# Cross-attention stage: every fourth head's turned probabilities copied by DVE, behind the maximum of the pair two steps on

## The reference

```
qh, kh, vh = 16 heads of 32 features of layernorm(x), c, c      # 256 queries, 256 keys per sequence
scores = einsum('bhqd,bhkd->bhqk', qh, kh) / sqrt(32);  key > query is masked to -10000
attn   = softmax(scores);  out = einsum('bhqk,bhkd->bhqd', attn, vh)
x      = x + tanh(g_xattn[1]) * out
```

## Time and profile before

| | us |
|---|---|
| median of 3 runs | 2086.57 (2085.92 to 2087.85) |
| profiled execution, device time | 2086.45 |
| profiled execution, span of the trace | 2084.6 |
| `cross`: first PE transposes to the end of the last POOL addition | 1691.0 to 1904.2 |

### The profile page before, as it was taken

The page is one execution under the profiler, slowest core; times in us unless marked ns, Lnnn a source line. Parts: engine busy times, 40 slices in busy tenths (PEclk is TensorE's granted clock), DMA queues, the critical chain, the costliest instruction groups (busy, mean ns, idle before and its releaser), DMA issues. The chain is left out here.

```text
span 2084.6 us, 30601 instructions
## 1 busy us (share of the span) xinstructions
PE 1934.9 (93%) x10490; PEld 1481.0 (71%) x10490; DVE 1351.3 (65%) x2408; ACT 1080.1 (52%) x2590; POOL 430.7 (21%) x515
## 2 busy tenths in 40 slices
PE   6999889999999999969998999999989978886998
PEld 5888667777777777757887788887778855553454
DVE  6777577777777777744433655564655447885886
ACT  3333366666766666652313321223234238895998
POOL 1111144444444444410000000000000002222111
PEclk9999999999999999989999999999999989998999
DMA  6776953333332331137333221223386423331121
GB/s 251 260 260 216 327 146 112 81 92 94 100 89 84 92 81 31 32 112 251 132 121 111 68 75 41 66 56 121 104 297 236 146 78 103 116 98 52 38 55 46
DMA packets 209028, 253.76 MB, mean 122 GB/s; under 512 B 12246, under 2 KB 158822, under 8 KB 202476
## 3 DMA queue, kind: packets, MB, share of 16 engines
q1 hardware_dynamic: 208876, 251.82, 37.6%
HBM read 151.10 MB, written 100.68 MB: 121 GB/s over the span
## 5 line engine op out<-in xcount | busy, mean ns | idle before, releaser
L1082 DVE TENSOR_TENSOR queries_v_lo<-at_PT,queries_v_hi 128x512 fp32r<-128x512 f32 x224 | 154.8, 692 | 84.7 <-ACT queries_v_hi L991 84.7
L1062 DVE TENSOR_REDUCE at_nmax<-at_S 128x1 f32<-128x384 f32 (+1 forms) x256 | 152.5, 618 | 7.9 <-PE at_S L898 3.7
L991 ACT ACTIVATE queries_v_hi<-at_PT 128x512 fp32r<-128x512 f32 x224 | 134.9, 603 | 43.7 <-PE at_PT L905 43.7
L1757 ACT ACTIVATE gu_silu<-gu_G 128x512 f32<-128x512 f32 x64 | 38.0, 596 | 208.9 <-PE gu_G L103 184.9
L984 ACT ACTIVATE queries_kt_lo<-at_S,at_bias,at_rq 128x512 f32<-128x512 f32 x128 | 99.3, 785 | 62.9 <-DVE at_bias L1071 62.9
L1792 DVE TENSOR_TENSOR gu_h<-gu_silu,gu_U 128x512 f32<-128x512 f32 x64 | 43.5, 685 | 127.0 <-PE gu_U L103 79.3
L837 POOL TENSOR_TENSOR at_q<-at_by_cos,at_by_sin 128x512 f32<-128x512 f32 x64 | 82.4, 1288 | 208.0 <-DVE at_qv L1057 183.5
L984 ACT ACTIVATE queries_kt_hi<-at_S,at_bias,at_rq 128x384 f32<-128x384 f32 x128 | 85.9, 681 | 68.5 <-DVE at_bias L1071 61.3
L894 PE MATMUL at_S<-at_k_hi,at_q_hi 128*128 128x384 f32 (+1 forms) x256 | 110.3, 431 | 7.5 <-DVE at_q_lo L1087 7.5
L258 PE MATMUL down_Y<-down_w_hi,down_a_hi 128*128 128x512 f32 x256 | 101.9, 398 | 11.8 <-DVE d_y L1426 11.8
L848 POOL TENSOR_SCALAR queries_kt_lo<-queries_kt_lo,at_rsum 128x512 f32<-128x512 f32 x128 | 87.5, 697 | 87.5 <-DVE at_rsum L1077 87.5
(11 more groups left out here) (352 smaller groups left out, 5682.3 us busy)
## 6 DMA issues: line engine op xcount, KB each, us to landing
wide<-at_ot SPq DMA_DIRECT2D x64, 256.0 KB, 2.9
wide<-gu_h SPq DMA_DIRECT2D x64, 256.0 KB, 3.3
o_a<-wide SPq DMA_DIRECT2D x14, 1024.0 KB, 4.8
d_a<-wide SPq DMA_DIRECT2D x13, 1024.0 KB, 8.6
at_k_hi<-keys_hi SPq DMA_DIRECT2D x64, 128.0 KB, 3.2
at_k_lo<-keys_lo SPq DMA_DIRECT2D x64, 128.0 KB, 3.3
at_v_hi<-values_hi SPq DMA_DIRECT2D x64, 128.0 KB, 3.3
at_v_lo<-values_lo SPq DMA_DIRECT2D x64, 128.0 KB, 3.6
```

The lines of the kernel that those rows point to most:

```text
L991: act.activation(pt_hi[f % 4], bank_of("p", u, kb)[:], ACT.Copy).then_inc(pt_hi_done.sem, 1)
L1062: dve.tensor_reduce(nmax[:, s:s + 1], S[h][:, 0:blocks[u] * P], AX_X, ALU.max, negate=True).then_inc(max_done.sem, 1)
L1082: dve.tensor_tensor(pt_lo[f % 4], bank_of("p", u, kb)[:], pt_hi[f % 4].bitcast(F32), ALU.subtract).then_inc(pt_done.sem, 1)
```

## The change

ACT copies the odd heads' turned probabilities now in even steps only (heads with h % 4 = 1). Those of heads with h % 4 = 3 are copied by DVE, in odd steps, right behind `maximum` of that step and ahead of whatever else DVE does there. They count on a new counter `pt_fourth`; `kept` gives the right counter for a head, `turn_probs` waits for head h-2's, and `values` waits for both of its last heads' counters. PE's order is unchanged. In the diff below the fourth piece (with `-2` and the new `if`) is ACT's step, and the last two are new on DVE. The copied shape and data are the same, 32 of the 128 copies change their engine.

```
-        pt_done = mem.counter("pt_done", NU)
+        pt_done = mem.counter("pt_done", NU - NQ)
+        pt_fourth = mem.counter("pt_fourth", NQ)
...
+        def kept(turn, h):
+            return pt_fourth.at(turn, h // 4 + 1) if h % 4 == 3 else pt_done.at(turn, h + 1 - (h + 1) // 4)
...
             def turn_probs(turn, h):
-                pe.wait_ge(*pt_done.at(turn, h - 1))
+                pe.wait_ge(*kept(turn, h - 2))
...
             def values(turn, n):
-                pe.wait_ge(*pt_done.at(turn, 4 * n + 4))
+                pe.wait_ge(*kept(turn, 4 * n + 2))
+                pe.wait_ge(*kept(turn, 4 * n + 3))
...
                 for turn, p in at(-2):
-                    keep_probs(turn, 2 * p + 1)
+                    if p % 2 == 0:
+                        keep_probs(turn, 2 * p + 1)
...
+            def keep_probs(turn, h):
+                dve.wait_ge(*PT_full.at(turn, h + 1))
+                dve.wait_ge(*PV_done.at(turn, h // 4 - 1))
+                dve.tensor_copy(pt[h % 8][:], PT[h % 2][:, 0:3 * P]).then_inc(pt_fourth.sem, 1)
...
                 for a in at(0):
                     maximum(*a)
+                for turn, p in at(-2):
+                    if p % 2 == 1:
+                        keep_probs(turn, 2 * p + 1)
```

More of the change, by code:

```diff
@@ L2210, in _ @@
         def _(dve):
-            for s in (x_kept[1], v1_kept, masked_done, max_done, sums_done, rsum_done, gain_done, apart_gained, o_done):
+            for s in (x_kept[1], v1_kept, pt_fourth, masked_done, max_done, sums_done, rsum_done, gain_done, apart_gained, o_done):
                 s.start(dve)
```

## The result

| kernel | median, us | runs | profiled execution |
|---|---|---|---|
| before | 2086.74 | 4 (2085.92 to 2087.85) | 2086.45, span 2084.6 |
| changed | 2107.43 | 4 (2105.49 to 2109.79) | 2108.97, span 2107.2 |

The changed kernel is slower by 20.7 us, a ratio of 1.0099 (95% interval 1.0086 to 1.0112). The forecast was 2091.3 with a range up to 2094.0: the sign was right and the size four times too small.

The account below looks back on a forecast made before the run. Stages follow each other, so only `cross` counts: short hand-overs bound plain steps, DVE part of each batch. +0.52 or +0.88 a batch in seven batches gave +3.6 or +6.2, taken as 4.9: 2086.45 + 4.9 = 2091.3, range 2086.0 to 2094.0.

Parts of the forecast that it names:

- the last sentence of the sum: Everything outside the priced terms (semaphores, POOL's work, the DMAs) was said to be unmoved, so it added nothing.
- step 1's to step 4's scores: DVE's copy adds 0.45 up to step 2's mask, ACT's lost copy gives back 0.21: +0.24 a batch, 9.13 to 9.37.
- steps 5 and 6, mask ahead of POOL: If the mask goes first in step 4, POOL's second addition stalls step 5's mask: 6.76 for 6.04, +0.72 a batch.
- steps 5 and 6, POOL ahead of the mask: If POOL goes first in step 4, the mask stands 1.15 there: steps 5 and 6 take 6.40 for 6.04, +0.36.
- steps 7 and 0: This pair of steps, across the batch boundary, falls from 5.67 to 5.59 us: -0.08 a batch.
- the ring: Hand-overs over two steps through scores, mask, reduce, DVE's copy, PE and ACT's copy: 5.59 us against 5.58, 0.0 a pair.
- the release of PE by DVE's copy: From the end of DVE's copy to PE's next odd turn, priced at 0.15 us.
- The meeting: In step 4 POOL's addition and DVE's mask become ready within 0.03 us; either goes first, taken half and half.
- (a): Rival: mask first in step 4, POOL's second addition behind step 5's mask; batch nearly 0, 2086.2; 0.18 together with (d).
- (b): Rival: PE's turn needn't wait for DVE, so 32 odd steps each keep 0.49: -15.7 us, 2070.8; chance 0.07.
- (c): Rival: DVE's copy starts after the reduce and holds DVE 0.684; pairs and DVE-bound part lengthen: 12.7, 2099.2; chance 0.07.
- (d): Rival: no visible change, as (a) and the main case mix over batches, 2087 to 2089; 0.18 together with (a).

Follow-up runs that it names:

- the memset: The kernel before with a 128x576 memset on DVE behind each odd maximum, nobody waiting for it, all copies left on ACT: 2108.52 us, 1.0111 of before.

## Why the prediction was wrong

The time between the two kernels, over steps 8 to 63, is 189.10 - 168.63 = 20.47 us. With both idle stretches filled it is 170.77. At full clock throughout the kernel before would need 6 x 23.87 + 20.74 = 163.96. So: the path 170.77 - 163.96 = 6.81 us, the half clock 189.10 - 170.77 = 18.33, less 168.63 - 163.96 = 4.67 that the kernel before lost to the clock itself. That is 20.47. The 6.81 is a bound from above: about 1.0 of it is half clock in the last batch's step 6 (5.64), which wasn't filled, and 0.35 a single first step of 3.44. An estimate of the path by batches is 6 x 0.71 and 1.2 for the last one, 5.4 us.

**The step that failed** is the last sentence of the sum, that all else is unmoved, which puts PE's clock at nothing without a reason. It was taken that PE's matmuls, whose list and order the change leaves alone, keep their durations. I had read the batch "at full clock" and priced everything by it. The profile had warned of this: PE idled 1.06 us in step 3, in the other batches behind the first 0.98 to 1.06, and the kernel before had slow steps of its own (4.12, 4.60 and 3.83 us at places where 2.79 or 3.03 is usual). The second of them came right behind such a stretch, as this view of the kernel before shows; the other two are first steps of a batch, behind 0.77 and 0.67 us of idling:

```profile
1759.94:1764.54 4.60, 4.60 (x35) 2.80 (x35) 3.32 (x3) 3.15 (x13) 1.27 (x1) 0.63 0.17 69
```

The working showed that the maximum would come 0.45 later in step 3. It should have asked what PE does meanwhile: idle 1.5 instead of 1.06. In its place the runs showed 18.3 us of half clock, which went when the two idle stretches were filled. No rival had the clock in it, which is why the range ended at 2094.0.

**The path itself was nearly right**, and its steps can be checked in the batches with full clock:

| term | predicted | measured |
|---|---|---|
| the copy on DVE | 0.55, next after 0.45 | 0.546, next after 0.46 |
| step 1's to step 4's scores | 9.37 | 9.38 |
| steps 5 and 6, mask ahead of POOL | 6.76 | 2.10 + 4.57 = 6.67 |
| steps 5 and 6, POOL ahead of the mask (ten matmuls in step 3) | 6.40 | 3.02 + 3.18 = 6.20 |
| steps 7 and 0 | 5.59 | 2.40 + 3.09 = 5.49 |
| a batch against 23.87 | +0.52 or +0.88 | +0.71 |

The path costs about 5.4 us against the 4.9 of the sum. That they lie so close is partly luck: the 4.9 is the mean of two branches, only the dearer one happened, and that one was priced at 6.2. The median with both stretches filled, 2089.79 against 2086.42 beside it (+3.4), is no test of the 4.9 either, since that kernel before still loses 4.67 us to the clock in its trace.

The term that was too dear in the ring is the release of PE by DVE's copy, taken as 0.15. In a plain pair of the changed kernel the copy ends at 1712.84 + 0.55 = 1713.39 and PE starts 0.05 later; the rest of the ring is as summed, so it takes 5.49 and not 5.59:

```profile
1712.84 0.55 DVE L2249 COPY x_pt<-x_PT 128x384 f32<-128x384 f32 x1
...
1713.44 0.55 PE L2092 MATMUL x_PT<-c_ident,x_prob 128*128 128x128 f32 x3 [0.57 <-DVE x_pt L2249]
```

**POOL or the mask.** The meeting was called even. In the batches at full clock the mask always went first in step 4 (0.70 at 1874.99), and its stall moved to step 5, where it takes 1.63. So of the two branches it was the dearer one.

```profile
1874.99 0.70 DVE L2240 COPY_PREDICATED x_S<-x_after,x_masked 128x512 f32<-128x512 int32 x1
1875.02 1.79 POOL L2036 TENSOR_TENSOR x_y<-x_o,x_xe 128x512 f32<-128x512 f32 x1 [3.24 <-DVE x_o L2270]
...
1877.82 1.28 POOL L2036 TENSOR_TENSOR x_y<-x_o,x_x 128x512 f32<-128x512 f32 x1 [1.00 <-DVE x_o L2270]
```

**A smaller miss.** Step 1 was to shrink to 2.4 like the other odd steps. It stays at 2.79, because PE has `second_values` there (1.02 us at 1866.36, and the next scores start at 1867.32); the path of steps 1 to 3 hides it.

**The rivals.** (a) The collision vanishes: no, it moved. (b) ACT's copies were the path: no; the odd plain step falls to 2.06 and the even one rises to 3.43, 5.49 together against 5.58. (c) A later release: no; 0.546 and 1.14, as in the main case. (d) no: +0.71 a batch at full clock. What happened was none of them.

## What to carry to other kernels

When a change makes PE wait longer, even by half a microsecond, look at how long PE is then idle in one piece, and whether the kernel already has stretches of half clock behind such pieces; price the matmuls that follow at half clock as one case of the prediction. Whether it is the clock can be tested: put matmuls of no use into the idle stretch, no longer than it, and see whether the kernel gets faster. Look for a second stretch before believing a partial answer; here filling one with five gave back 6.6 us and filling both 17.6. Moving work onto DVE, which was busy for 137.41 of 168.63 us, costs nothing in the steps where it waits and the full price in the few steps where it is last, so the share over the stage says little.

## What the runs showed of the hardware

- With the copy in step 1 alone, PE idled 1.45 to 1.52 us in one piece once per batch, and the step behind it took 4.55 to 5.54 instead of 3.03, at half clock, in seven of seven batches. In the kernel before the stretch was 0.98 to 1.06 and this happened in one of seven (4.60). The changed kernel has two such stretches per batch (1.51 to 1.60 in step 3, 1.28 to 1.47 in step 6); behind the first, step 4 was slow in six of seven. The Trainium skill, page "TensorE: Matmul & The Clock Gate", section "Part 1: The HAM clock gate", describes a gate that goes by how busy PE has been recently and knows the same two levels, and the trace agrees (0.50 and 1.00).
- What exactly makes the clock fall stays open, and the length of the last idle stretch doesn't decide it alone. 1.61 us was once followed by a step at full clock (the memset, step 4 of 3.03), 1.06 by half clock in two of seven batches (DVE copying in steps 3, 5 and 7), and 0.67 to 0.77 in front of a batch's first step by half clock twice in the kernel before. Step 6 of the changed kernel, with its idling of up to 1.47, took 4.38 to 4.57 in five of six batches; once step 3 was filled it took 5.34 to 6.00 in four of six.
- `keep_awake`'s matmul of 128x128 in fp32 is two rows and 0.24 us at full clock (20 rows in 2.40 us), not 0.12.
- POOL's addition and DVE's mask held each other up both ways: the one that comes second waits. The addition takes 1.79 us when it starts 0.03 behind the mask, and 1.27 when it is ahead.
